# Expert stage of a routed feed-forward kernel: order of ScalarE's silu and VectorE's output operations in a step

## The chip, the cores and the metric

The kernel runs on one core of one Trainium2 chip. The metric is the device time of one execution in microseconds. Before the change it is 377.3 us in the median of 3 runs (376.8 to 378.77). The five engines of the core have queues of their own, which are worked off in order, and meet only by semaphores: TensorE (PE; its weight loads are shown as PEld), VectorE (DVE), ScalarE (ACT), GpSimd (POOL) and SyncE (SP). A name with a q behind it, such as ACTq, is an engine's sequencer.

## The reference

The input is x, 4096 rows of 256 columns. It is normalized, goes through a spiking attention block (s) and, in parallel, through a feed-forward block with 8 experts; each row uses one expert, the nearest of 8 centroids. The stage that the change touches computes the second of these and joins the two:

```python
for e in range(N_EXPERTS):
    h = jnp.einsum('bsd,dh->bsh', xn, up_w[e])
    a, g = jnp.split(h, 2, axis=-1)
    y = jnp.einsum('bsh,hd->bsd', a * jax.nn.silu(g), down_w[e])
    out = jnp.where((ids == e)[..., None], y, out)
return out + skip
...
g = _silu(_L0_ffn_ref(xn, ...))
x = x + s * g
```

up_w is 8 x 256 x 1024, down_w is 8 x 512 x 256, all in float32.

## The kernel before

The first part (up to some 165 us of the span) normalizes, projects, does the attention and sorts the rows by expert. The rest is the expert stage. Rows are taken by expert in 39 tiles of 128 (ST = 39, enough for 4096 rows in groups of 8 experts that are each filled up to whole tiles). For tile s, GpSimd gathers the rows into one of four buffers row_a (x and normalized x, `gather_a`, L1514) and the attention's rows into row_s (`gather_s`, L1520), by indirect DMA, and scatters the result e_o to the output (`scatter`, L1564). Its queue per tile is gather_a(s), gather_s(s-2), scatter(s-4); gather_a(s) waits until the output of tile s-4 is computed (semaphore o_done), since it reuses its buffer.

float32 products are made from high and low halves of each operand, in three groups of matmuls: high x high, high x low and low x high. ScalarE makes the high half (a copy), VectorE the low half (a subtraction).

The stage is written as steps k, and the four compute engines each go through their own `step_c(k)`. In step k

- TensorE does `turn_rows(k)` (2 transposes of row_a, L677), `expert_down(k-2)` (12 matmuls, L724: 4 with d_hi and e_hh, 4 with d_hi and e_hl, 4 with d_lo and e_hh), `turn_hidden(k-1)` (4 transposes of e_h, L688), and `expert_up(k)` (12 matmuls, L705: gate half, then value half).
- ScalarE does e_xh, the high half of the turned rows (L909); reads the expert's number into a register (`value_load`, L927); d_hi, the high half of tile k-1's down weights (L938), after the down matmuls of tile k-2 are done (down_done), since there is one buffer; silu of the gated sum e_z of tile k-2, in place (L945); e_hh, the high half of tile k-1's hidden values (L919); silu of the gate half of tile k (L953, into e_h).
- VectorE does e_xl (L1315); reads the expert's number (L1365); e_z, the sum of tile k-2's down product and its rows, called the gated sum here since its silu is the gate of the spikes (L1370, semaphore z_done); d_lo (L1374) after d_hi; e_hl (L1377) after e_hh; `finish`, the output of tile k-2 in two operations (L1354 multiplies the silu by row_s, L1356 adds x; o_done); e_h, the product of gate and value (L1385). In steps 2 and 3 `finish` stands behind e_h instead.

Each engine's order is the order of the code; nothing is planned at run time. The last tile's down weights have a buffer of their own, d_end (L959).

Of the kernel before, what the change touches and what calls it, by code (L numbers as in the profile page):

```python
# [25 lines left out]
ACT = mybir.ActivationFunctionType  # L26
# [61 lines left out]
def build(nc, x, wq, wk, wv, wo, vectors, centroids, up_w, down_w, consts, blocks, eye, out):  # L88
    with ExitStack() as ctx:
# [136 lines left out]
        def over_weights(name, n, shape, dt=F32):  # L226
            made = []
            for k in range(n):
                made.append(place(f"{name}{k}", shape, dt, at=over[0])[0])
                over[0] += 4 * shape[1] * (shape[2] if len(shape) > 2 else 1)  # L230
            return made
# [6 lines left out]
        e_h, e_z = over_weights("e_h", 2, [P, HID]), over_weights("e_z", 2, [P, D])  # L238
# [62 lines left out]
        eht_done, eht_kept, down_done, z_done, g_done, sg_done, o_done = (  # L301
            sem("eht_done"), sem("eht_kept"), sem("down_done"), sem("z_done"), sem("g_done"), sem("sg_done"), sem("o_done"))

        def after(eng, s, count):

            if not isinstance(count, int) or count > 0:
                eng.wait_ge(s, count)
# [445 lines left out]
        def _(act):  # L753
# [150 lines left out]
            def turned_high(k, i):  # L904

                s = k + 4 * i
                act.wait_ge(ext_done, s + 1)
                after(act, up_done, 2 * (s - 1))
                act.activation(e_xh[k % 2][:, :, :], bank[7][:, 0:D].rearrange("p (c n) -> p c n", c=DC),  # L909
                               ACT.Copy).then_inc(ext_high, 1)  # L910
# [5 lines left out]
            def hidden_high(k, i):  # L916

                act.wait_ge(eht_done, k + 4 * i)
                act.activation(e_hh[1 - k % 2][:, :, :], bank[6][:, :].rearrange("p (c n) -> p c n", c=HC),  # L919
                               ACT.Copy).then_inc(hid_high, 1)  # L920

            def step_c(k, i):
                s, b = k + 4 * i, k % 2
                if 0 < k < ST:
                    turned_high(k, i)
                if 0 <= k - 1 < ST - 1:
                    e = act.value_load(expert[0:1, bass.ds(s - 1, 1)], min_val=0, max_val=E - 1)  # L927
                if 0 <= k - 1 < ST:

                    if k == 1:  # L930
                        act.wait_ge(wo_sq, NT)
                    if k < 4:
                        act.wait_ge(down_ready, e + 1)
                    elif k == 4:
                        act.wait_ge(down_ready, E)
                    if k < ST:
                        after(act, down_done, s - 1)
                        act.activation(d_hi[:, :, :], down_sb[:, bass.ds(e, 1), :, :].rearrange("p a c n -> p (a c) n"),  # L938
                                       ACT.Copy).then_inc(d_high, 1)
                if k == ST:  # L940
                    hidden_high(k, i)
                if k >= 2:

                    act.wait_ge(z_done, s - 1)
                    act.activation(e_z[b][:, :], e_z[b][:, :], ACT.Silu).then_inc(g_done, 1)  # L945
                if 0 <= k - 1 < ST - 1:
                    hidden_high(k, i)
                if k < ST:
                    act.wait_ge(up_done, 2 * s + 1)
                    after(act, eht_done, s - 1)  # L950
                    if k == 1:
                        act.wait_ge(s_made, NT)
                    act.activation(e_h[b][:, :], bank[1][:, :], ACT.Silu,  # L953
                                   scale=row_a[k % 4][:, D + 1:D + 2]).then_inc(gate_done, 1)
                if k == ST - 1:

                    e = act.value_load(expert[0:1, k:k + 1], min_val=0, max_val=E - 1)
                    act.wait_ge(up_done, 2 * ST)
                    act.activation(d_end[:, :, :], down_sb[:, bass.ds(e, 1), :, :].rearrange("p a c n -> p (a c) n"),  # L959
                                   ACT.Copy).then_inc(d_high, 1)  # L960

            for k in range(ST + 2):
                step_c(k, 0)
# [3 lines left out]
        def _(dve):  # L967
# [320 lines left out]
            def output_spikes(k, i):  # L1288
                c, s = k + 2 * i, k % 2
                if c >= 2:  # L1290
                    dve.wait_ge(s_put[s], 16 * (c // 2))
                for pair in range(2):
                    dve.wait_ge(wo_rs, c + 1)
                    for n in range(2):
                        tl = 2 * pair + n
                        V.scalar_tensor_tensor(s_out[s][:, tl, :], bank[2 + 2 * s + pair][:, n * D:(n + 1) * D],
                                               tile_of(rs, c * CH + tl)[:, 3:4], thr[:, 3 * D:4 * D],
                                               ALU.mult, ALU.is_ge).then_inc(s_made, 1)
# [11 lines left out]
            def turned_low(k, i):  # L1310

                s = k + 4 * i
                dve.wait_ge(ext_high, s + 1)
                after(dve, up_done, 2 * (s - 1))
                V.tensor_tensor(e_xl[k % 2][:, :, :], bank[7][:, 0:D].rearrange("p (c n) -> p c n", c=DC),  # L1315
                                e_xh[k % 2][:, :, :].bitcast(F32), ALU.subtract).then_inc(ext_kept, 1)
# [28 lines left out]
            def finish(k, i):  # L1345

                s, b = k + 4 * i, k % 2

                dve.wait_ge(g_done, s - 1)
                if k - 2 >= 4:  # L1350
                    dve.wait_ge(sent[(k - 2) % 4], 16 * ((k - 2) // 4 + i))
                dve.wait_ge(got_s[(k - 2) % 4], 16 * ((k - 2) // 4 + i + 1))
                o = e_o[(k - 2) % 4]
                V.tensor_tensor(o[:, :], e_z[b][:, :], row_s[(k - 2) % 4][:, :], ALU.mult).then_inc(sg_done, 1)  # L1354
                dve.wait_ge(sg_done, s - 1)
                V.tensor_tensor(o[:, :], o[:, :], row_a[(k - 2) % 4][:, D + 2:2 * D + 2], ALU.add).then_inc(o_done, 1)  # L1356

            def step_c(k, i):
                s, b = k + 4 * i, k % 2
                if 0 < k < ST:  # L1360
                    turned_low(k, i)
                if k == 1:
                    output_spikes((NCH - 1) % 2, NCH // 2 - 1)
                if 0 <= k - 1 < ST:
                    e = dve.value_load(expert[0:1, bass.ds(s - 1, 1)], min_val=0, max_val=E - 1)  # L1365
                if 0 <= k - 2 < ST:

                    dve.wait_ge(down_done, s - 1)
                    after(dve, sg_done, s - 3)
                    V.tensor_tensor(e_z[b][:, :], bank[2 + b][:, 0:D], row_a[(k - 2) % 4][:, 0:D], ALU.add).then_inc(z_done, 1)  # L1370
                if 0 <= k - 1 < ST:

                    dve.wait_ge(d_high, s)
                    V.tensor_tensor(d_lo[:, :, :], down_sb[:, bass.ds(e, 1), :, :].rearrange("p a c n -> p (a c) n"),  # L1374
                                    (d_hi if k < ST else d_end)[:, :, :].bitcast(F32), ALU.subtract).then_inc(d_low, 1)
                    dve.wait_ge(hid_high, s)
                    V.tensor_tensor(e_hl[1 - b][:, :, :], bank[6][:, :].rearrange("p (c n) -> p c n", c=HC),  # L1377
                                    e_hh[1 - b][:, :, :].bitcast(F32), ALU.subtract).then_inc(eht_kept, 1)
                if k > 3:
                    finish(k, i)  # L1380
                if k < ST:

                    dve.wait_ge(gate_done, s + 1)
                    dve.wait_ge(up_done, 2 * s + 2)
                    V.scalar_tensor_tensor(e_h[b][:, :], bank[0][:, :], row_a[k % 4][:, D + 1:D + 2], e_h[b][:, :],  # L1385
                                           ALU.mult, ALU.mult).then_inc(act_done, 1)
                if 2 <= k < 4:
                    finish(k, i)

            for k in range(ST + 2):  # L1390
                step_c(k, 0)
# [262 lines left out]
```

## Time and profile before

| | |
|---|---|
| median of 3 runs | 377.3 us |
| the profiled execution | 374.0 us, of which the span (first to last instruction) is 372.2 us |
| TensorE clock granted | 0.996 of full speed (2.4 GHz) in the mean |
| busy in the span | PE 354.3 us, PEld 300.9, DVE 303.8, ACT 240.3, POOL 231.7 |
| chain that ended last, by engine | PE 59%, DVE 14%, DMA 11%, issue 6%, ACT 5%, POOL 3% |
| its largest member in the expert stage | up matmuls L705 12%, down matmuls L724 11%, gather of row_a 10% |

The profile shows one execution. A row of its views has a start and a duration in us, the engine, the line of the code, the operation, and what it writes and reads. In brackets behind it stands how long the engine was idle before, and what released it. PE's ends are modelled, since matmuls overlap, so PE's busy time hides short waits; the weight loads show them. "issue" is time in which an engine waited for nothing that the profile shows. The chain that ended last is followed back from the last instruction, at each step to what released it.

### The profile page before, as it was taken

To read this page: it belongs to the slowest core of one execution; us is meant where nothing else is said; L and a number is where in the kernel's file an instruction comes from. 1 tells how busy PE (TensorE), PEld (TensorE's weight loads), DVE (VectorE), ACT (ScalarE), POOL (GpSimd) and SP (SyncE) were. 2 spreads that over 40 slices of the span, in tenths; PEclk is the share of its full clock that TensorE was granted. 3 is DMA by queue.
4 is the path that set the end of the run, shared out by engine and by line. 5 is a ranking of instruction groups with operands and counts; after the bars stand their busy time and mean duration, and the time that the engine had idled before them with its cause. 6 is when DMAs were issued, how large, how long until landed. Compare 5 with 4: busy or idle time off the path is not lost.

```text
span 372.2 us, 8971 instructions
## 1 busy us (share of the span) xinstructions
PE 354.3 (95%) x2463; PEld 300.9 (81%) x2464; DVE 303.8 (82%) x782; ACT 240.3 (65%) x645; POOL 231.7 (62%) x295
## 2 busy tenths in 40 slices
PE   7989999999999999988999999999999999999991
PEld 4778888888877888867788888888888888888881
DVE  5979999998879778989877778777778887777883
ACT  5498889889955677874555555565555565655561
POOL 4877778788640249674666666666666667666662
PEclk9999999999999999999999999999999999999998
DMA  7696767755189631664133112333222332322100
GB/s 224 188 304 182 210 180 232 244 157 146 67 165 228 199 107 57 199 192 121 41 91 100 55 58 84 90 85 100 65 73 82 90 98 87 90 78 65 37 17 0
DMA packets 31927, 45.46 MB, mean 122 GB/s; under 512 B 4162, under 2 KB 25859, under 8 KB 31765
## 3 DMA queue, kind: packets, MB, share of 16 engines
q1 hardware_dynamic: 25248, 29.73, 27.5%
q0 software_dynamic: 6416, 15.26, 14.2%
q8 instruction: 12, 0.20, 0.3%
q14 instruction: 23, 0.18, 0.2%
q10 hardware_dynamic: 228, 0.10, 0.1%
HBM read 36.84 MB, written 15.63 MB: 141 GB/s over the span
## 4 chain that ended last, share of the span: by engine, by line
PE 59%; DVE 14%; DMA 11%; issue 6%; ACT 5%; POOL 3%; ACTq 0%; POOLq 0%; DVEq 0%
PE bank L508 16%; PE bank L705 12%; PE bank L724 11%; DMA row_a<-rows_a,slot_id 10%; ACT d_hi L938 3%; PE bank L622 3%; PE bank L583 3%; PE bank L677 2%; DVE d_lo L1374 2%; PE bank L688 2%; DVE e_hl L1377 2%; PE bank L487 2%; PE bank L586 2%; DVE e_o L1356 1%; DVE up_lo L1304 1%
## 5 line engine op out<-in xcount | busy, mean ns | idle before, releaser
L1374 DVE TENSOR_TENSOR d_lo<-down_sb,d_hi 128x1024 fp32r<-128x1024 f32 x38 | 46.5, 1225 | 31.6 <-ACT d_hi L938 31.6
L938 ACT ACTIVATE d_hi<-down_sb 128x1024 fp32r x38 | 40.3, 1060 | 43.6 <-PE bank L724 39.7
L1514 POOL DMA_INDIRECT row_a<-rows_a,slot_id x39 | 40.4, 1036 | 44.4 <-DVE e_o L1356 43.6
L1564 POOL DMA_INDIRECT out_x<-e_o,slot_id x39 | 44.6, 1143 | 16.7 <-issue 11.8
L705 PE MATMUL bank<-up_hi,e_xh 128*128 x156 | 51.9, 414 | 0.0
L1520 POOL DMA_INDIRECT row_s<-rows_s,slot_id x39 | 39.8, 1022 | 16.4 <-issue 11.6
L705 PE MATMUL bank<-up_hi,e_xl 128*128 x156 | 48.5, 392 | 1.0 <-DVE e_xl L1315 1.0
L705 PE MATMUL bank<-up_lo,e_xh 128*128 x156 | 48.4, 391 | 0.0
L909 ACT ACTIVATE e_xh<-bank 128x256 fp32r<-128x256 f32 x39 | 15.0, 385 | 39.5 <-PE bank L677 39.5
L831 ACT ACTIVATE junk<-bank 128x256 bf16<-128x256 f32 x96 | 35.4, 379 | 2.8 <-PE bank L508 2.7
L705 PEld LDWEIGHTS bank<-up_hi,e_xl 128*128 128x128 f32 x156 | 29.2, 188 | 7.8 <-DVE e_xl L1315 1.4
L508 PE MATMUL bank<-w_hi,x_hi 128*128 128x264 f32 (+1 forms) x128 | 35.4, 358 | 0.0
L705 PEld LDWEIGHTS bank<-up_lo,e_xh 128*128 128x128 f32 x156 | 29.3, 188 | 6.2
L508 PE MATMUL bank<-w_lo,x_hi 128*128 128x264 f32 (+1 forms) x128 | 33.1, 340 | 0.0
L508 PE MATMUL bank<-w_hi,x_lo 128*128 128x264 f32 (+1 forms) x128 | 32.9, 338 | 0.0
L1438 POOL TENSOR_TENSOR rs<-pv,half_neg 128x3 f32 (+1 forms) x32 | 27.2, 850 | 7.5 <-POOL pv L1435 7.5
L705 PEld LDWEIGHTS bank<-up_hi,e_xh 128*128 128x128 f32 x156 | 26.6, 189 | 3.5
L1385 DVE SCALAR_TENSOR_TENSOR e_h<-bank,row_a,e_h 128x512 f32<-128x512 f32 x39 | 29.0, 745 | 0.2
L953 ACT ACTIVATE e_h<-bank,row_a 128x512 f32<-128x512 f32 x39 | 26.7, 685 | 2.6 <-PE bank L705 2.6
L724 PE MATMUL bank<-d_hi,e_hh 128*128 128x256 f32 x152 | 27.2, 301 | 0.0
L1377 DVE TENSOR_TENSOR e_hl<-bank,e_hh 128x512 fp32r<-128x512 f32 x39 | 26.7, 684 | 0.0
L773 ACT ACTIVATE xn<-xs,nmr,inv_std 128x256 f32<-128x256 f32 x32 | 19.2, 601 | 10.9 <-DVE nmr L1124 6.6
(241 smaller groups left out, 972.7 us busy)
## 6 DMA issues: line engine op xcount, KB each, us to landing
up_raw<-in_up_w SPq DMA_DIRECT2D x16, 512.0 KB, 4.3
rows_a<-xn SPq DMA_DIRECT2D x32, 129.0 KB, 2.4
rows_a<-in_x SPq DMA_DIRECT2D x8, 512.0 KB, 12.1
xs<-in_x SPq DMA_DIRECT2D x7, 512.0 KB, 4.4
down_sb<-in_down_w SPq DMA_DIRECT2D x5, 512.0 KB, 6.0
rows_s<-s_out SPq DMA_DIRECT2D x8, 256.0 KB, 3.0
down_sb<-in_down_w SPq DMA_DIRECT2D x6, 256.0 KB, 4.0
blk_tab<-in_blocks SPq DMA_DIRECT2D x1, 1024.0 KB, 6.2
```

What stands on the lines that cost most here:

```text
L508: last = pe.matmul(to[:, 0:c1 - c0], left[s][:, c, :], right[:, c, c0:c1], start=(n == 0 and c == 0), stop=(n == 2 and c == DC - 1))
L705: last = pe.matmul(bank[half][:, :], left[k % 2][:, c, :], w[:, c, half * HID:(half + 1) * HID], start=(n == 0 and c == 0), stop=(n == 2 a ...
L724: last = pe.matmul(bank[2 + k % 2][:, 0:D], left[k % 2][:, c, :], w[:, c, :], start=(n == 0 and c == 0), stop=(n == 2 and c == HC - 1))
L831: act.activation(junk[n][:, :], src, ACT.Square, accum_out=tile_of(ss, u)[:, n:n + 1]).then_inc(squared, 1)
L938: act.activation(d_hi[:, :, :], down_sb[:, bass.ds(e, 1), :, :].rearrange("p a c n -> p (a c) n"), ACT.Copy).then_inc(d_high, 1)
L1374: V.tensor_tensor(d_lo[:, :, :], down_sb[:, bass.ds(e, 1), :, :].rearrange("p a c n -> p (a c) n"), (d_hi if k < ST else d_end)[:, :, :].b ...
L1377: V.tensor_tensor(e_hl[1 - b][:, :, :], bank[6][:, :].rearrange("p (c n) -> p c n", c=HC), e_hh[1 - b][:, :, :].bitcast(F32), ALU.subtract ...
L1385: V.scalar_tensor_tensor(e_h[b][:, :], bank[0][:, :], row_a[k % 4][:, D + 1:D + 2], e_h[b][:, :], ALU.mult, ALU.mult).then_inc(act_done, 1)
L1438: G.tensor_tensor(tile_of(rs, t)[:, 0:3], pv[:, s, 0:3], halves, ALU.pow).then_inc(rs_done, 1)
L1514: G.indirect_dma_start(row_a[s % 4][:, :], None, rows_a, bass.IndirectOffsetOnAxis(ap=slot_id[:, s:s + 1], axis=0), bounds_check=N - 1, oo ...
L1520: G.indirect_dma_start(row_s[s % 4][:, :], None, rows_s, bass.IndirectOffsetOnAxis(ap=slot_id[:, s:s + 1], axis=0), bounds_check=N - 1, oo ...
L1564: G.indirect_dma_start(out, bass.IndirectOffsetOnAxis(ap=slot_id[:, s:s + 1], axis=0), e_o[s % 4][:, :], None, bounds_check=N - 1, oob_is_ ...
```

## The change

In ScalarE's step, the silu of tile k-2's gated sum moves ahead of the register read and of the copy of the down weights. In VectorE's step, `finish` moves from behind e_hl to right behind the gated sum, from step 4 on; in steps 2 and 3 it stays behind e_h. What is computed, and with how many instructions, is unchanged. In the last steps (k = ST and k = ST + 1) the same order holds, so silu stands ahead of the last `hidden_high` there.

```diff
@@ ScalarE, step_c
                 if 0 < k < ST:
                     turned_high(k, i)
+                if k >= 2:
+
+                    act.wait_ge(z_done, s - 1)
+                    act.activation(e_z[b][:, :], e_z[b][:, :], ACT.Silu).then_inc(g_done, 1)
                 if 0 <= k - 1 < ST - 1:
                     e = act.value_load(expert[0:1, bass.ds(s - 1, 1)], min_val=0, max_val=E - 1)
                 if 0 <= k - 1 < ST:
...
                                        ACT.Copy).then_inc(d_high, 1)
                 if k == ST:
                     hidden_high(k, i)
-                if k >= 2:
-
-                    act.wait_ge(z_done, s - 1)
-                    act.activation(e_z[b][:, :], e_z[b][:, :], ACT.Silu).then_inc(g_done, 1)
                 if 0 <= k - 1 < ST - 1:
                     hidden_high(k, i)
@@ VectorE, step_c
                     V.tensor_tensor(e_z[b][:, :], bank[2 + b][:, 0:D], row_a[(k - 2) % 4][:, 0:D], ALU.add).then_inc(z_done, 1)
+                if k > 3:
+                    finish(k, i)
                 if 0 <= k - 1 < ST:
 
                     dve.wait_ge(d_high, s)
...
                                     e_hh[1 - b][:, :, :].bitcast(F32), ALU.subtract).then_inc(eht_kept, 1)
-                if k > 3:
-                    finish(k, i)
                 if k < ST:
```

## Rows read from the trace of the kernel before

**Rows 1.** Waits, 200 to 350 us: who waited for whom; us in total, times, longest

```profile
POOL row_a L1514 <- DVE e_o L1356: 36.9, 30, 1.3
...
DVE d_lo L1374 <- ACT d_hi L938: 25.7, 30, 0.9
...
PEld bank L677 <- DMA row_a<-rows_a,slot_id: 8.5, 19, 0.6
```

**Rows 2.** Chain that ended last: start us, us, what

```profile
251.30 0.03 POOLq L1514
...
252.04 3.52 DMA row_a<-rows_a,slot_id
```

**Rows 3.** Timeline (start us, us, engine, line, operation): third down matmul groups, 3 of 39

```profile
191.05 0.64 PE L724 MATMUL bank<-d_lo,e_hh 128*128 128x256 f32 x4
...
357.05 0.64 PE L724 MATMUL bank<-d_lo,e_hh 128*128 128x256 f32 x4
...
361.70 0.64 PE L724 MATMUL bank<-d_lo,e_hh 128*128 128x256 f32 x4
```

**Rows 4.** Timeline of TensorE's weight loads of e_hl, two steps in a row

```profile
256.24 0.55 PEld L724 LDWEIGHTS bank<-d_hi,e_hl 128*128 128x128 f32 x4
...
261.09 0.55 PEld L724 LDWEIGHTS bank<-d_hi,e_hl 128*128 128x128 f32 x4
```

**Rows 5.** Timeline of one step; in brackets the idle time before and its releaser

```profile
256.84 0.64 PE L724 MATMUL bank<-d_lo,e_hh 128*128 128x256 f32 x4
...
257.52 0.42 DVE L1370 TENSOR_TENSOR e_z<-bank,row_a 128x256 f32<-128x256 f32 x1 [0.41 <-PE bank L724]
257.61 1.06 ACT L938 ACTIVATE d_hi<-down_sb 128x1024 fp32r x1 [1.14 <-PE bank L724]
...
258.57 0.40 ACT L945 ACTIVATE e_z<-e_z 128x256 f32<-128x256 f32 x1
...
258.81 1.22 DVE L1374 TENSOR_TENSOR d_lo<-down_sb,d_hi 128x1024 fp32r<-128x1024 f32 x1 [0.86 <-ACT d_hi L938]
258.88 0.58 ACT L919 ACTIVATE e_hh<-bank 128x512 fp32r<-128x512 f32 x1
...
259.95 0.68 DVE L1377 TENSOR_TENSOR e_hl<-bank,e_hh 128x512 fp32r<-128x512 f32 x1
...
260.55 0.41 DVE L1354 TENSOR_TENSOR e_o<-e_z,row_s 128x256 f32<-128x256 f32 x1
...
261.00 0.42 DVE L1356 TENSOR_TENSOR e_o<-e_o,row_a 128x256 f32<-128x256 f32 x1
...
261.34 0.74 DVE L1385 SCALAR_TENSOR_TENSOR e_h<-bank,row_a,e_h 128x512 f32<-128x512 f32 x1
```

**Rows 6.** Timeline behind the last tile's down matmuls

```profile
365.49 0.42 DVE L1370 TENSOR_TENSOR e_z<-bank,row_a 128x256 f32<-128x256 f32 x1 [0.16 <-PE bank L724]
365.95 0.42 ACT L945 ACTIVATE e_z<-e_z 128x256 f32<-128x256 f32 x1 [2.00 <-DVE e_z L1370]
...
366.39 0.42 DVE L1354 TENSOR_TENSOR e_o<-e_z,row_s 128x256 f32<-128x256 f32 x1 [0.48 <-ACT e_z L945]
```

**Rows 7.** ScalarE's register read L927 (ns min/median/max, first and last start); last instance; timeline

```profile
L927 ACTq TENSOR_LOAD <-expert x38: 273/278/492, 169.8 to 356.3; - x38
...
L927 ACTq SEQ_ASSERT  x1: 18/18/18, 356.8 to 356.8; - x1
...
356.29 0.38 ACT L909 ACTIVATE e_xh<-bank 128x256 fp32r<-128x256 f32 x1 [0.89 <-PE bank L677]
```

**Rows 8.** Timeline of the first steps

```profile
175.27 0.65 PE L724 MATMUL bank<-d_lo,e_hh 128*128 128x256 f32 x4
...
179.21 0.75 DVE L1385 SCALAR_TENSOR_TENSOR e_h<-bank,row_a,e_h 128x512 f32<-128x512 f32 x1
...
184.82 0.44 PE L677 MATMUL bank<-ident,row_a 128*128 128x128 f32 x2 [0.87 <-DMA row_a<-rows_a,slot_id]
```

## The prediction

> **What bounds the kernel now.** Read in this order: the waits of the expert stage, the chain of work that ended last, then one step of that stage in order of time. The waits [rows 1] say that TensorE's weight loads stood still 8.5 us in 150 us for the gathered rows (19 of the 30 steps), that GpSimd in turn waits for VectorE's last output operation before it may issue that gather, and that VectorE waits 0.86 us in each step for ScalarE's copy of the down weights. The chain [rows 2] joins these: output written, gather issued, 3.5 us of DMA, transposes. It closes over two steps and costs 5.03 us a step: TensorE's third group of down matmuls starts at 191.05 and 33 steps later at 357.05, lasts 0.64 both times [rows 3], so T, the end of a tile's down matmuls, goes from 191.69 to 357.69, and 166.0/33 = 5.03. TensorE's own work in a step is less: the load of e_hl weights recurs from 256.24 to 261.09, 4.85 us, in a step without a gather wait [rows 4]. So at most 0.18 us a step is to be had by freeing the gather, some 6 us in 33 steps.
>
> **A step in order of time**, with T = 256.84 + 0.64 = 257.48 [rows 5]: gated sum e_z at T+0.04, d_hi at +0.13, silu of e_z at +1.09, d_lo at +1.33, the copy e_hh at +1.40, e_hl at +2.47, ending +3.15, the output operations to +3.95, e_h at +3.86. The e_hl is wanted by TensorE at 261.09, T+3.61 [rows 4]: 0.46 us of slack. That slack is the number to watch.
>
> **Part 1: silu ahead of the down-weight copy (ScalarE).** Nothing is added or removed; what changes is that d_hi, with all that is queued behind it (hidden copy e_hh, gate silu), now stands behind a wait for VectorE's e_z. In today's order silu never waits for it. The last tile shows the bare handover: e_z at 365.49, silu at 365.95, 0.46 [rows 6]. So silu starts at T+0.50, and d_hi can't be earlier. By occupation of the engine alone it would start 0.31 after silu (258.57 to 258.88, the next operation behind a silu) [rows 5].
>
> But the diff puts silu ahead of another instruction too: the read of the tile's expert number into a register (L927), whose value d_hi's address needs. Today it lies in the 1.14 us in which ScalarE idles before d_hi, and costs nothing. Its load takes 0.278 us in the middle case, 0.492 at the longest of 38; in the last instance it starts at 356.3 and the closing check at 356.8, lasting 0.018 [rows 7]. And it starts at 356.3 with the e_xh operation at 356.29, which had waited 0.89 us [rows 7]: it didn't run ahead of a waiting operation. So it will start with silu at T+0.50, not before. Load to check 0.50, check 0.02, a handover of some 0.03 (estimate), and 0.09 for d_hi's own address operation and issue (d_hi starts at T+0.13 though its wait ended at T; e_z behind the same event at T+0.04): 0.64 from silu to d_hi. Bounds: 0.31 if the read hides, 0.64 + 0.21 = 0.85 if every load takes 0.492. I take 0.64, the middle load. d_hi then starts at T+1.14 instead of T+0.13. Queued behind it are e_hh, which ends near T+2.7 and is wanted at T+3.14 (258.88 + 0.58 today, against 0.47 ahead of 261.09), and the gate silu, which e_h needs only at T+4.1; who waits for d_hi itself is VectorE's d_lo.
>
> The Trainium skill (DMA: Bandwidth & Descriptors, "Latency and other measured facts") gives a tensor_load a floor of about 600 ns; this trace disagrees with 0.278. By that figure a step would be 0.32 us longer yet, and the sum some 12 us higher.
>
> **Part 2: output right behind the gated sum (VectorE).** The two operations wait for silu (start +0.44 in [rows 6]), start 0.45 apart and take 0.43; behind the second the next operation may start 0.34 later (261.00 to 261.34) [rows 5]. That is T+0.50+0.44 = +0.94, then +1.39, free at +1.73. They fit into VectorE's wait for d_hi, which lasts until T+1.14+1.20 = +2.34, so they cost nothing where they stand, and their 0.8 us vanish ahead of e_h. If d_hi came before +0.53, they would be what d_lo waits for. The output is done at about +1.82 instead of +3.95, so the gather is issued 2.1 us sooner and its wait (at most 0.6 us at a time) goes. Queued behind these waits are d_lo, e_hl and e_h. The moved operations' other waits (an earlier scatter's end, the row_s gather) have two steps of lead and aren't late. GpSimd has 1.2 us of idle time ahead of each gather [rows 1], so its queue stays below the step.
>
> **What is late next: e_hl.** Behind T+1.14, start to start: d_hi to d_lo 1.20 (257.61 to 258.81), d_lo to e_hl 1.14 (258.81 to 259.95), e_hl itself 0.68 [rows 5], handover to the weight load 0.05 (estimate from VectorE's to ScalarE's, 0.46 less the 0.42 of e_z [rows 6]), and from that load to T again 1.24 (256.24 to 257.48) [rows 4, 5]. The sum of the new loop:
> 0.04 + 0.46 + 0.64 + 1.20 + 1.14 + 0.68 + 0.05 + 1.24 = 5.45 us a step.
> e_hl is ready at T+4.21; TensorE wants it at T+3.61 and waits 0.60 in every step. The two ways agree: 4.85 + 0.60 = 5.45. The other orders keep slack: e_h starts 0.60 behind e_hl (259.95 to 260.55, the next operation behind an e_hl [rows 5]), at T+4.1, ends +4.85 and is wanted only at the new T+5.45; e_xl and VectorE's read of the expert number follow it and end before T+5.4.
>
> **The sum.** Steps between the tiles of T = 191.69 and 357.69: 33 x (5.45 - 5.03) = 13.9 us. The first steps: for tiles 0 and 1 the output stays behind e_h in the code, and e_h moves from T+3.3 (179.21 against 175.27 + 0.65) to T+4.1, so both first gathers come 0.8 later, the second also by the 0.6 of its own step; both are waited for already (0.87 at 184.82) [rows 8]: +1.4. The step from 357.69 to 362.34 [rows 3] becomes 5.45: +0.8. The last: the diff puts two output operations and silu ahead of d_lo where nothing was waited for; e_z to T again is 0.04 + 0.46 + 0.44 + 0.45 + 0.34 + 1.14 + 0.68 + 0.05 + 0.72 (four matmuls and the first one's delay) = 4.3 instead of 365.45 - 362.34 = 3.1 (365.49 less 0.04) [rows 3, 6]: +1.2. What follows is unchanged. Together 13.9 + 1.4 + 0.8 + 1.2 = 17.3. The profiled execution took 374.0 us (span 372.2), the median is 377.3; I keep that distance: 391.3 for a profiled one, **394.6 us** for the median.
>
> **Rivals.** *Read hidden.* If the register read ran past the waiting silu, d_hi would start 0.31 behind silu: loop 5.12. 33 x 0.09 = 3.0, first steps 0.8, then 0.5 and 1.2: 5.5, or 382.8 us. Against it is the start with e_xh in [rows 7]. The Trainium skill (Perfetto Trace Analysis, "Per-engine timelines") has the sequencer free for the next instruction once an operation is pushed into its wait queue, ahead of its semaphore; by that rule the read could pass. The rows speak against it for this read. Chance 0.08.
>
> *Long reads.* If next to VectorE's and TensorE's own reads or silu's traffic each load takes 0.492: 5.66 a step, 36 x 0.21 = 7.6 more: 402 us. Only the rare load does so now. Chance 0.12.
>
> *Faster: the gather was the only loop that counts.* The freed gather takes the stage to TensorE's pace if e_hl is ready by T+3.61: 33 x (4.85 - 5.03) = -6, with up to 1.2 of loss at the end, about 372 us. It decides at a loop of 5.03: that needs 0.42 of the 5.45 gone, more than a hidden read's 0.33, so also shorter handovers around silu. For it speaks only that VectorE now waits 0.86 for d_hi, which output work fills; but that work was never ahead of e_hl. Chance 0.06.
>
> *Forecast*, e_hl as the new wait with the middle read: 0.74, 391 to 398 by itself.
>
> **Chances and range.** A change under 0.5% (1.9 us) can't be told from none here. Slower holds the forecast, the long and the hidden read: 0.94, less 0.02 for a mixture near no change. Faster 0.05, same 0.03, slower 0.92. The range goes from 388 (a loop of 5.25, between the bounds of the read) to 403 (long reads); it leaves out the hidden read and the faster case, 0.14, and little more.
>
> **What would show it.** TensorE's weight load of e_hl waits about 0.6 us for VectorE's L1377 group in nearly every step; the waits for row_a are gone from the middle of the stage; silu waits for e_z; ScalarE idles some 0.3 us between silu and d_hi with no releaser; output done near T+1.8; steps of 5.45. It is wrong if d_hi follows silu at 0.31, if row_a is still waited for, or if a step is under 5.2.

## The result, and the profile after

The changed kernel takes 395.32 us in the median (394.43 to 395.49, 4 runs) against 378.03 for the kernel before (376.8 to 378.8, 4 runs): a ratio of 1.0466, 95% interval 1.043 to 1.0503. It is slower by 17.3 us. The profiled execution took 395.21 us with a span of 393.3; before, 374.0 and 372.2.

The waits of the changed kernel between 200 and 350 us, who waited for whom, us in total, times, longest:

```profile
ACT e_z L929 <- DVE e_z L1370: 54.9, 25, 3.7
POOL row_a L1514 <- issue: 23.5, 25, 0.9
PEld bank L724 <- DVE e_hl L1379: 15.4, 27, 0.9
DVE d_lo L1376 <- ACT d_hi L942: 14.1, 27, 0.8
...
ACT d_hi L942 <- issue: 6.5, 27, 0.5
```

TensorE's weight loads no longer wait for row_a: the line of [rows 1] is gone from this stretch. They wait for e_hl instead, 27 times, 0.57 us each. GpSimd's gather waits for the output in only 2 of 27 steps (5.2 us in all, 36.9 before); in the other 25 it has "issue" ahead of it, so the output is early enough. And there is a new line, ScalarE's d_hi after "issue", 0.24 us in each of 27 steps. One step in order of time, to be laid beside [rows 4, 5]:

```profile
255.59 0.64 PE L724 MATMUL bank<-d_lo,e_hh 128*128 128x256 f32 x4
...
256.27 0.42 DVE L1370 TENSOR_TENSOR e_z<-bank,row_a 128x256 f32<-128x256 f32 x1 [0.32 <-PE bank L724]
...
256.73 0.42 ACT L929 ACTIVATE e_z<-e_z 128x256 f32<-128x256 f32 x1 [2.11 <-DVE e_z L1370]
...
257.18 0.43 DVE L1354 TENSOR_TENSOR e_o<-e_z,row_s 128x256 f32<-128x256 f32 x1 [0.48 <-ACT e_z L929]
...
257.37 1.06 ACT L942 ACTIVATE d_hi<-down_sb 128x1024 fp32r x1 [0.22 <-issue]
...
257.64 0.43 DVE L1356 TENSOR_TENSOR e_o<-e_o,row_a 128x256 f32<-128x256 f32 x1
...
258.58 1.23 DVE L1376 TENSOR_TENSOR d_lo<-down_sb,d_hi 128x1024 fp32r<-128x1024 f32 x1 [0.51 <-ACT d_hi L942]
...
258.85 1.85 POOL L1514 DMA_INDIRECT row_a<-rows_a,slot_id  x1 [0.94 <-issue]
...
259.72 0.68 DVE L1379 TENSOR_TENSOR e_hl<-bank,e_hh 128x512 fp32r<-128x512 f32 x1
260.32 0.74 DVE L1385 SCALAR_TENSOR_TENSOR e_h<-bank,row_a,e_h 128x512 f32<-128x512 f32 x1
260.46 0.53 PEld L724 LDWEIGHTS bank<-d_hi,e_hl 128*128 128x128 f32 x4 [0.54 <-DVE e_hl L1379]
```

With T = 256.23: e_z at +0.04, silu at +0.50, d_hi at +1.14, d_lo at +2.35, e_hl at +3.49, e_hl's weight load at +4.23, and from e_z to the next e_z 5.44 us. Each of the eight terms of the forecast's loop is met within 0.03 us.

The sum over the stage is less tidy. The starts of e_z mark T at its corners (T is 0.04 earlier):

```profile
194.16 0.42 DVE L1370 TENSOR_TENSOR e_z<-bank,row_a 128x256 f32<-128x256 f32 x1 [0.59 <-PE bank L724]
...
201.79 0.42 DVE L1370 TENSOR_TENSOR e_z<-bank,row_a 128x256 f32<-128x256 f32 x1 [2.48 <-remote]
...
376.33 0.42 DVE L1370 TENSOR_TENSOR e_z<-bank,row_a 128x256 f32<-128x256 f32 x1 [0.33 <-issue]
...
381.77 0.42 DVE L1370 TENSOR_TENSOR e_z<-bank,row_a 128x256 f32<-128x256 f32 x1 [0.66 <-PE bank L724]
...
386.61 0.42 DVE L1370 TENSOR_TENSOR e_z<-bank,row_a 128x256 f32<-128x256 f32 x1 [1.31 <-PE bank L724]
```

From the corner of 191.69 before to 194.12 after, the first steps cost 2.4 us. The 33 steps took 182.2 us against 166.0: 16.2. The next step took 5.44 instead of 4.65 (0.8), the last 4.84 instead of 3.11 (1.7). Together 21.1, the difference of the two spans.

### The profile page after: what moved, and what is told of

Same layout as the page of the kernel before. It is cut to its first block, busy times and chain, and to the rows that moved or that the text cites. A ratio compares the mean times of both kernels' runs of the same rounds, so it can differ in the third digit from the quotient of the medians.

```text
span 393.3 us, 8971 instructions
## 1 busy us (share of the span) xinstructions
PE 361.8 (92%) x2463; PEld 305.4 (78%) x2464; DVE 308.1 (78%) x782; ACT 242.8 (62%) x645; POOL 252.7 (64%) x295
## 4 chain that ended last, share of the span: by engine, by line
PE 49%; DVE 22%; ACT 12%; issue 10%; POOL 2%; ACTq 2%; DVEq 1%; DMA 1%; another core or an unknown queue 1%; POOLq 0%
PE bank L508 16%; PE bank L724 10%; ACT d_hi L942 8%; DVE d_lo L1376 7%; DVE e_hl L1379 5%; PE bank L705 4%; DVE e_z L1370 3%; PE bank L622 3%; PE bank L583 3%; ACT e_z L929 2%; PE bank L487 2%; PE bank L586 2%; PE bank L439 1%; ACTq L931 1%; DVE up_lo L1304 1%
## 5 line engine op out<-in xcount | busy, mean ns | idle before, releaser
L1514 POOL DMA_INDIRECT row_a<-rows_a,slot_id x39 | 65.9, 1689 | 40.2 <-issue 28.7
L929 ACT ACTIVATE e_z<-e_z 128x256 f32<-128x256 f32 x39 | 16.3, 418 | 84.9 <-DVE e_z L1370 70.1
L1564 POOL DMA_INDIRECT out_x<-e_o,slot_id x39 | 41.7, 1069 | 20.6 <-issue 11.4
L724 PE MATMUL bank<-d_hi,e_hl 128*128 128x256 f32 x152 | 27.8, 305 | 13.0 <-DVE e_hl L1379 12.3
L724 PEld LDWEIGHTS bank<-d_hi,e_hl 128*128 128x128 f32 x152 | 20.4, 188 | 20.1 <-DVE e_hl L1379 19.0
L1354 DVE TENSOR_TENSOR e_o<-e_z,row_s 128x256 f32<-128x256 f32 x39 | 16.6, 425 | 17.9 <-ACT e_z L929 16.5
L1370 DVE TENSOR_TENSOR e_z<-bank,row_a 128x256 f32<-128x256 f32 x39 | 16.6, 425 | 15.8 <-PE bank L724 12.4
```

What stands on the lines that cost most here:

```text
L724: last = pe.matmul(bank[2 + k % 2][:, 0:D], left[k % 2][:, c, :], w[:, c, :], start=(n == 0 and c == 0), stop=(n == 2 and c == HC - 1))
L1514: G.indirect_dma_start(row_a[s % 4][:, :], None, rows_a, bass.IndirectOffsetOnAxis(ap=slot_id[:, s:s + 1], axis=0), bounds_check=N - 1, oo ...
L1564: G.indirect_dma_start(out, bass.IndirectOffsetOnAxis(ap=slot_id[:, s:s + 1], axis=0), e_o[s % 4][:, :], None, bounds_check=N - 1, oob_is_ ...
```

## The experiments

Four kernels (e1 to e4) ran beside a kernel before of 377.7 us (7 runs), four (e5 to e8) beside 374.7 (13 runs), two beside 374.5 (7 runs). Ratios are taken within a group; across groups the length of a step compares better than the time. A step is the mean from e_z to e_z in the middle of the stage.

**Each half of the change alone.** e1 takes VectorE's part back:

```diff
-                if k > 3:
-                    finish(k, i)          # behind e_z
...
+                if k > 3:
+                    finish(k, i)          # behind e_hl, as before
```

> ScalarE's part of the change alone: silu and then the register read ahead of d_hi, VectorE's output back behind e_hl. Theory (e_hl comes late over e_z, silu, read, d_hi, d_lo): the loop of 5.45 us a step stays whole, and the output is done near T+5.0, so the gather of row_a is late as well: 5.03 + 0.05 + 4.13 from output to transposes + 1.88 to T = 11.1 us for two steps, 5.5 a step; 395 to 398 us. Rival (the place of the output operations makes the loss): about 378 us, as before.

Measured: 404.99 us, ratio 1.0718 (1.0641 to 1.0795). The rival fell, but the size was missed: the step is 5.82 us, not 5.5. The waits between 200 and 350 us, and one step of it:

```profile
PEld bank L677 <- DMA row_a<-rows_a,slot_id: 11.9, 25, 0.9
PEld bank L688 <- DVE e_h L1385: 11.4, 26, 0.5
```

```profile
258.31 0.42 DVE L1356 TENSOR_TENSOR e_o<-e_o,row_a 128x256 f32<-128x256 f32 x1
...
258.58 0.64 PE L724 MATMUL bank<-d_lo,e_hh 128*128 128x256 f32 x4
258.65 0.74 DVE L1385 SCALAR_TENSOR_TENSOR e_h<-bank,row_a,e_h 128x512 f32<-128x512 f32 x1
259.31 0.41 DVE L1315 TENSOR_TENSOR e_xl<-bank,e_xh 128x256 fp32r<-128x256 f32 x1
...
259.65 0.41 DVE L1370 TENSOR_TENSOR e_z<-bank,row_a 128x256 f32<-128x256 f32 x1
...
260.09 0.42 ACT L929 ACTIVATE e_z<-e_z 128x256 f32<-128x256 f32 x1 [2.09 <-DVE e_z L1370]
```

The matmuls of the tile end at 258.58 + 0.64 = 259.22, but e_z starts at 259.65, with no idle time ahead of it: VectorE itself isn't free. The loop closes without TensorE: e_z, silu 0.45, d_hi 0.65, d_lo 1.20, e_hl 1.14, then two outputs, e_h, e_xl and e_z again 0.60 + 0.45 + 0.34 + 0.66 + 0.34: 5.83. Silu's place in ScalarE's queue turned VectorE's whole queue into a ring: each e_z now waits, by way of silu and d_hi, on the e_z before it. So once silu is ahead, the moved output isn't the harm; it takes 0.79 us out of this ring (5.83 to 5.04) and leaves the loop over e_hl as the bound.

e2 is the other half: VectorE's order of the change, ScalarE's of before.

> VectorE's part alone: output right behind e_z, ScalarE as before (d_hi, then silu). Theory: the output waits for a silu that starts at T+1.09, so the two operations start at T+1.53 and T+1.98 and d_lo at T+2.32 instead of T+1.33, while d_hi is ready at T+1.19. Sum 2.32 + 1.14 + 0.68 + 0.05 + 1.24 = 5.43 us a step by another way, 393 to 396 us, with VectorE's idle time ended by silu and not by d_hi. Rival (all of the loss is ScalarE's order): the gather is freed at no cost, 371 to 378 us.

Measured: 390.6 us, ratio 1.0337 (1.0264 to 1.0409), the step 5.42. The step is as worked out; the median is 2.4 us under the lower end, and the stop on VectorE described at the end, 2.2 us in the changed kernel, is missing here. One step on VectorE:

```profile
262.87 0.42 DVE L1370 TENSOR_TENSOR e_z<-bank,row_a 128x256 f32<-128x256 f32 x1 [0.31 <-PE bank L724]
264.36 0.43 DVE L1354 TENSOR_TENSOR e_o<-e_z,row_s 128x256 f32<-128x256 f32 x1 [1.06 <-ACT e_z L945]
264.82 0.42 DVE L1356 TENSOR_TENSOR e_o<-e_o,row_a 128x256 f32<-128x256 f32 x1
265.16 1.22 DVE L1376 TENSOR_TENSOR d_lo<-down_sb,d_hi 128x1024 fp32r<-128x1024 f32 x1
```

The idle time is ended by silu now, 1.06 us, and d_lo stands behind the output with no wait left, 2.29 us after e_z instead of 1.29 in [rows 5]. Either half alone is enough to bring the step to 5.4 or more. Their costs don't add up: both delay the same d_lo (to 2.3 us behind e_z), and the second half takes the output out of the ring of e1.

**The register read.** e3 moves it ahead of silu in the changed kernel; e10 puts a second one behind silu.

```diff
+                if 0 <= k - 1 < ST - 1:
+                    e = act.value_load(...)
                 if k >= 2:
 
                     act.wait_ge(z_done, s - 1)
                     act.activation(e_z[b][:, :], e_z[b][:, :], ACT.Silu).then_inc(g_done, 1)
-                if 0 <= k - 1 < ST - 1:
-                    e = act.value_load(...)
```

> The changed kernel with the register read of the expert's number ahead of silu instead of behind it. Theory (the read lies on the path with 0.33 us a step): silu to d_hi falls from 0.64 to 0.31, the step from 5.45 to 5.12, 36 steps x 0.33 = 12 us less, 383 to 384 us. Rival (d_hi waits for the engine or for silu's end, and the read is beside it): 395 us, as the changed kernel.

Measured: 383.53 us, ratio 1.0153 (1.0081 to 1.0226), the step 5.10 (the profiled execution has in it a stop of 2.6 us, described at the end). ScalarE's rows, of e3:

```profile
262.95 0.42 ACT L931 ACTIVATE e_z<-e_z 128x256 f32<-128x256 f32 x1 [1.78 <-DVE e_z L1370]
263.28 1.04 ACT L942 ACTIVATE d_hi<-down_sb 128x1024 fp32r x1
```

> The changed kernel with the register read between silu and d_hi done twice; the second value is not used. Theory (the read's 0.50 us lies bare on the path once silu's 0.31 us of occupation is used up): silu to d_hi 0.64 + 0.50 = 1.14, the step 5.45 + 0.50 = 5.95, 36 steps give 18 us: about 413 us. Rival (the idle time between silu and d_hi is something else that the read only sits in): 395 us.

Measured: 413.38 us (2 runs), ratio 1.1027 (1.0976 to 1.1078), the step 5.98. ScalarE's rows, of e10:

```profile
263.40 0.42 ACT L929 ACTIVATE e_z<-e_z 128x256 f32<-128x256 f32 x1 [2.40 <-DVE e_z L1372]
264.57 1.06 ACT L944 ACTIVATE d_hi<-down_sb 128x1024 fp32r x1 [0.76 <-issue]
```

From silu to d_hi: 0.33 with no read between, 0.64 with one, 1.17 with two. The second read costs 0.53; the first only 0.31, since 0.33 would have passed anyway. That is what "issue" ahead of d_hi meant.

**Which wait of TensorE.** e4 leaves both queues of the change alone and has TensorE use e_hl last, as it already does for the last tile:

```diff
-                if k == ST - 1:
-                    parts = (parts[0], parts[2], parts[1])
+                parts = (parts[0], parts[2], parts[1])
```

> The changed kernel with TensorE's down matmuls in the order high x high, low weights x high, high weights x low for every tile, so that e_hl is wanted one group of four later (0.48 us). Theory: four instead of eight matmuls follow e_hl, the step falls by 0.48 to 4.97, 36 steps give 17 us, about 378 us; TensorE still waits for e_hl, by 0.1 us. Rival (the loss is in TensorE's clock, 0.990 after against 0.996 before, or in VectorE's own occupation, which this order doesn't change): 393 us or more.

Measured: 381.63 us (379.45 to 384.06), ratio 1.0111 (1.0021 to 1.0201) where the changed kernel has 1.0466. The rival is out; the fastest of these executions, 379.45 us, even had a mean granted clock of 0.988, below the 0.990 of the changed kernel. The time is 3.6 us over the 378 expected; the stop described at the end took 1.9 in the profiled execution. The step is 5.03, not 4.97: with e_hl out of the way the ring on VectorE that e1 had laid bare is next, 5.04 as worked out above. Its mark is e_z with no idle time ahead of it:

```profile
261.03 0.74 DVE L1384 SCALAR_TENSOR_TENSOR e_h<-bank,row_a,e_h 128x512 f32<-128x512 f32 x1
261.69 0.41 DVE L1314 TENSOR_TENSOR e_xl<-bank,e_xh 128x256 fp32r<-128x256 f32 x1
262.02 0.41 DVE L1369 TENSOR_TENSOR e_z<-bank,row_a 128x256 f32<-128x256 f32 x1
```

e5 has both mends, e3's and e4's.

> The changed kernel with both mends, the register read ahead of silu and e_hl wanted one group later. Theory: the e_hl loop falls to 5.10 - 0.48 = 4.62, VectorE's own ring (e_z, silu, d_hi, d_lo, e_hl, e_h, e_xl, e_z: 0.46 + 0.32 + 1.18 + 1.14 + 0.60 + 0.66 + 0.34) to 4.70, both under TensorE's own 4.85, so the step is 4.85: 35 x 0.25 = 9 us less than with the read first alone, about 374.5 us, and TensorE waits for nothing in the middle of the stage. Rival (another wait, such as GpSimd's queue, whose gather operation now takes 1.87 instead of 1.03 us, keeps the step above 5.0): 380 us or more.

Measured: 370.8 us, ratio 0.9906 (0.9873 to 0.9938), the step 4.84. Between 200 and 350 us its waits have no line in which TensorE waits for anyone. The stage runs at TensorE's own pace. The step was as expected, the time 3.7 us lower; the kernel before is 3.0 us lower in this group too, and e3's stop on VectorE (at the end) is missing, so the two groups can't be compared closer than that.

**What bound the kernel before.** Three kernels built on it. e6 puts `finish` between d_lo and e_hl and has e4's order on TensorE; e7 has that order alone; e8 has one wait more:

```diff
                         after(act, down_done, s - 1)
+                        if k >= 2:
+                            act.wait_ge(z_done, s - 1)
                         act.activation(d_hi[:, :, :], ...)
```

> The kernel before with the output operations between d_lo and e_hl, and e_hl wanted one group later; ScalarE as before. Theory (before the change the gather's wait for the output is all that keeps the step above TensorE's work): output done at T+3.35 instead of T+3.95, the gather's loop 0.3 us a step shorter, 4.75; e_hl ends at T+3.94 and is wanted at T+4.09; step 4.85, 33 x 0.18 = 6 us less than before, about 371.5 us. Rival (e_hl, with 0.15 us of slack, comes late after all, or the gather isn't what waits): 377 us or more.

> Control: the kernel before, with only the order of TensorE's down matmuls changed, e_hl wanted 0.48 us later. Theory: e_hl wasn't late before, the gather loop (5.03 us a step) is untouched, so nothing changes, 376 to 379 us. Rival (e_hl was part of the wait before the change too): less than 375 us.

> The kernel before with one wait more: d_hi also waits for e_z. Order and work are unchanged. Theory: the bare handover moves d_hi from T+0.13 to T+0.59, e_hl's end from T+3.15 to T+3.61, which uses up its slack, and the output with it to T+4.41; the gather's loop over two steps grows by 0.46, the step to about 5.27: 35 x 0.24 = 8 us more, about 386 us, with row_a as TensorE's wait. Rival (0.46 us of slack hides it): 378 us.

Measured: e6 371.07 us, ratio 0.9899 (0.9877 to 0.9921); e7 374.94, 1.0002 (0.9985 to 1.0018); e8 386.45, 1.0315 (1.0293 to 1.0337). The waits of e6, of e7 and of e8 on row_a, same stretch:

```profile
PEld bank L677 <- DMA row_a<-rows_a,slot_id: 0.7, 1, 0.7
```

```profile
PEld bank L677 <- DMA row_a<-rows_a,slot_id: 8.8, 20, 1.0
```

```profile
ACT d_hi L940 <- DVE e_z L1372: 52.8, 29, 2.4
...
PEld bank L677 <- DMA row_a<-rows_a,slot_id: 13.0, 27, 0.9
```

With the output 0.6 us earlier the gather's wait falls from 8.8 to 0.7 us and the kernel gains 3.6 us, less than the 6 expected: its step is 4.90, not 4.85 (the views show no wait that makes up these 0.05, and their cause stays open), and its last two steps are together 0.8 longer than in e7, since the output stands ahead of e_hl there too. e_hl's slack alone (e7) changes nothing. e8 shows that a bare wait for e_z, with the order of before, costs 11.7 us: it delays d_hi, d_lo, e_hl and with them the output. The 8 us expected were too few: the step is 5.34 on average, where the gather's loop was put at 5.27. VectorE's ring closes in 5.32 in this order (0.59 + 1.20 + 1.14 + 0.60 + 0.45 + 0.34 + 0.66 + 0.34), most steps are 5.32 or 5.33, and e_z shows idle time ahead of it in only 5 of 39 tiles. So here the ring sets the step, and TensorE's wait for row_a, 0.48 us each time, stands beside it.

**A better kernel.** e5 loses time where silu ahead of d_hi helps nobody: in the first two steps and at the end.

```diff
-                if k >= 2:                          # silu ahead of d_hi
+                if 4 <= k < ST:
...
+                if 2 <= k < 4 or k >= ST:           # silu where it stood before
...
-                if k > 3:                           # output right behind e_z
+                if 3 < k < ST or k == ST + 1:
...
+                if k == ST:                         # output behind e_hl
```

> The kernel of e5 (read first, e_hl wanted one group later) with the order of the kernel before in the steps where silu or the output isn't waited for by anyone: ScalarE's silu behind d_hi in steps 2 and 3 and in the last two, VectorE's output behind e_hl in step ST. Theory: the last step falls from 4.36 to 3.13 us, the first ones give back about 1.2 (6.46 + 5.71 against 6.06 + 4.86 in e6), the rest stays at 4.84: 2 to 3 us under e5's 370.8, 368 to 369 us. Rival (the ends of the stage are set by the gathers alone, whatever this order): 370.8 us.

Measured: 368.9 us (368.25 to 371.03), ratio 0.986 (0.9816 to 0.9903). The last step fell from 4.36 to 3.00. Its median is the lowest of these kernels, though the interval of its ratio overlaps those of e5 and e6. It has the idea of the change in it: silu ahead, output behind e_z, once the read and e_hl are out of the way.

## Why the prediction was right

The forecast was 394.6 us in 388 to 403; measured 395.3.

*What bounds now.* Right: e7 leaves the gather's wait and the time alone, e6 takes the wait away and gains, though 3.6 us where 6 were thought to be had.

*Part 1, 0.46 and 0.64.* Right, and the two are shown apart: from e_z to silu it is 0.46 in the trace after (256.27 to 256.73), and e8 shows that such a wait alone slows the kernel; e3 and e10 price the read. The value chosen between the bounds, 0.64 (trace after: 256.73 to 257.37), rested on the three rows of [rows 7]. The load's median stayed 0.278 us with silu beside it. The rival of a read that passes the waiting silu, which the Trainium skill's order of events would allow (Perfetto Trace Analysis, "Per-engine timelines"), didn't occur: the last load of the trace after starts at 376.8, with the silu at 376.79, ahead of which ScalarE had been idle for 2.12 us, and not before it. e3, in which the read stands ahead of silu, is what the rival described, with a step of 5.10 against its 5.12.

*Part 2, no cost beside the wait for d_hi.* Right in the full change: VectorE still waits 0.51 us for d_hi behind the output. The cover is real, and gone in e2: there the output delays d_lo by 1.0 us.

*What is late next.* Right: e_hl, 0.54 us in a step where 0.60 was worked out. The ready time was T+4.17 where T+4.16 followed from the terms.

*The sum* has the errors. The profiled execution was put at 391.3 and took 395.2. The first steps cost 2.4 instead of 1.4: the first e_z comes 0.3 later than before, and the next three steps are 0.9, 0.3 and 0.9 longer; which term was short stays open. The last one cost 1.7 instead of 1.2: the terms hold, but TensorE's last group took twice its time (see the clock at the end). And 2.2 us went to one stop of VectorE that nothing in the trace before announces. The 3.3 us between profile and median, taken over from the kernel before, were then not there: the changed kernel's profiled execution is its median. The two misses, 3.9 us too few and 3.3 too many, nearly cancel. So the step of 5.45 was predicted; that the median came within 0.7 us was luck.

*Left out of the forecast:* VectorE's ring. It is 5.04 in the changed kernel, under 5.45, so it decided nothing there, but it made the expectation of e1 too low by 7 us and more, and the steps of e4 and e8 0.06 and 0.07 longer than expected, over 2 us each in some 35 steps. The prediction checked that e_h and e_xl were in time; it didn't sum them as a loop of their own.

## What to carry to other kernels

An operation moved ahead in a queue carries its wait onto all that stands behind it; ask of each of those how much slack it has where it is used, not where it is made. Here 0.46 us of slack stood against a delay of 1.01 us. Count the instructions that don't show as busy, too: a register read that hides in idle time costs nothing until something with a wait is put ahead of it. Here it then made the step 5.44 instead of 5.10 (e3), while silu and the output moved without it made 5.10 of 5.03.

Where a queue waits for its own earlier result by way of another engine, sum the ring. Its mark in a trace is an operation that starts late with no idle time ahead of it.

## What the runs showed of the hardware

**GpSimd's indirect DMA operation is held up by some VectorE operations that run when it starts.** It takes 1.03 us (262.20 before), and 1.85 in the row of 258.85 above. There it starts while d_lo runs (258.58 to 259.81) and ends 0.89 us behind d_lo's end. In e1 a scatter took 1.90 us and ended 0.91 behind d_lo:

```profile
256.11 1.22 DVE L1374 TENSOR_TENSOR d_lo<-down_sb,d_hi 128x1024 fp32r<-128x1024 f32 x1 [1.88 <-ACT d_hi L942]
256.34 1.90 POOL L1564 DMA_INDIRECT out_x<-e_o,slot_id  x1 [0.31 <-issue]
```

The order of the starts matters. In the kernel before, the operation below runs when d_lo starts (258.81), with 0.42 us side by side, and isn't longer:

```profile
258.23 1.00 POOL L1520 DMA_INDIRECT row_s<-rows_s,slot_id  x1 [0.30 <-issue]
```

What the held ones have in common is a VectorE operation with both inputs in SBUF. e_o is another: in e4 a scatter starts at 258.00 beside e_o (257.88 to 258.30), takes 1.20 us and ends 0.90 behind it. The gather of 262.20 starts beside e_xl (262.00 to 262.41), which reads the matmuls' result, and takes 1.03. The Trainium skill (SBUF — State Buffer, "Who interferes with whom") says that a VectorE instruction with two SBUF inputs contends with a GpSimd instruction that reads SBUF. The traces agree with it for operations that start while such an instruction runs, by these numbers, and show no delay for one that started before it (258.23). In the changed kernel it cost nothing, since GpSimd had 0.94 us of idle time ahead of the gather.

**The clock at the end.** TensorE's last 4 matmuls took 1.22 us instead of 0.64. Ahead of them TensorE had waited twice, and the granted clock of the stretch (381 to 387 us) was 0.86, with 3.70 of 6 us busy; in the 6 us before it was 1.00. In the second view below each row has the stretch, its length, the busy time of TensorE, its weight loads, VectorE, ScalarE and GpSimd, then the granted clock:

```profile
383.27 0.71 PE L724 MATMUL bank<-d_end,e_hh 128*128 128x256 f32 x4 [1.10 <-ACT e_hh L919]
...
384.75 0.76 PE L724 MATMUL bank<-d_lo,e_hh 128*128 128x256 f32 x4 [0.77 <-DVE d_lo L1376]
...
385.35 1.22 PE L724 MATMUL bank<-d_end,e_hl 128*128 128x256 f32 x4
```

```profile
375.00:381.00 6.00, 5.38 (x32) 4.67 (x33) 4.65 (x9) 3.60 (x5) 3.10 (x3) 1.00 0.02 4
381.00:387.00 6.00, 3.70 (x23) 2.92 (x21) 3.51 (x7) 0.90 (x2) 1.20 (x1) 0.86 0.01 0
```

From 385.3 to 386.6 us alone the granted clock is 0.52, the lower of the two levels, 1.2 GHz: the last group took 1.9 times its duration at 2.4 GHz. The two waits alone don't decide it: in e3 TensorE waited 1.10 and 0.78 us at the same places, its last group took 0.76, and its last step 4.39, near the 4.3 of the forecast. Why the clock fell in time to slow this group in one and not in the other, these runs don't show.

**A stop of 2 us on VectorE.** In the changed kernel e_z of the fifth tile starts at 201.79, 2.2 us after its matmuls are done (199.57, from the row 198.93 + 0.64), with a releaser that the profile doesn't know ("remote"). e3 and e4 have it at the same operation (2.6 and 1.9 us), e5 and the others don't, though e5 has e4's and the changed kernel's order on VectorE. A 16 KB DMA on an instruction queue starts 0.1 us behind the operation in all three, but such a DMA starts 1.6 to 3.2 us behind the same operation in the others too, and without the stop it would be 2.0 to 2.7 us behind it in these three. The cause of the stop stays open.
